# Gram products of every second row chunk made in the GIN stage, and rings of four buffers in the ranking stage of a four-layer graph network

## Chip, cores and metric

The kernel runs on one core of one Trainium2 chip. The metric is the device time of one execution in microseconds; smaller is better. TensorE (PE), VectorE (DVE), ScalarE (ACT), GpSimd (POOL) and SyncE (SP) have instruction queues of their own and meet by semaphores; 16 DMA engines move data.

## What is computed

Four graph layers, each followed by a residual and a row normalisation, over x of 50000 nodes x 256 features and 12500 edges. The change concerns the first layer (GIN) only:

```python
msgs = edge_vals[:, None] * x[edge_col]
agg = jax.ops.segment_sum(msgs, edge_row, num_segments=n)
h = (1.0 + eps[0]) * x + agg
h = _bn_relu(h @ W1 + b1, g1, be1)      # mean and variance over all 50000 rows
```

The batch norm needs the mean and variance of h @ W1. The kernel gets both from the Gram matrix of h, the 256 x 257 sum over all rows of h-transposed times [h, 1], before the matrix product itself is made. With h = s*x + agg, where agg is not zero only in rows that an edge ends in, the Gram matrix is the sum of the products of s*x with itself (all rows, the costly part) and of corrections for the rows with edges.

## The kernel before

The program runs phase by phase, and all engines meet between two phases: setup, histogram, ranking (function rank, 140 to 594 us of the profiled execution), segments (597 to 628), GIN edges (gin_edges, 628 to 1107), moments, then the matrix products and the other three layers, which the change doesn't touch.

The rows of x are cut into NCH = 100 chunks of 500 rows (125 partitions x 4 rows x 256 floats, 512 KB), the edges into T = 100 tiles of 125.

**Ranking** does two things side by side in one loop of 100 steps. It sorts the edges by source and by destination: VectorE makes one-hots of the keys' digits (L481) and copies of the keys (L484), TensorE transposes them (turn, L540 and L541), looks up the running table (find, L552) and adds the tile to it (count_in, L561), ScalarE copies and rounds the table (L444, L450) and the transposed one-hots (L457), VectorE compares keys in the tile (L493), makes the table's rest (L518) and sums of the lookup (L502), and GpSimd scatters the records by two indirect DMAs (L179). And it walks over x: SyncE loads chunk t into xin (L423), ScalarE scales it by 1 + eps into xc (L464), SyncE stores xc as H (L429, to the scratch tensor XP), and TensorE adds the chunk's products to gram in PSUM (moments, L572): for each of its 4 rows a partition two matmuls, one of 257 columns and one, for the second half of the features, of 129; the missing quarter is the transpose of another and is added once at the end (L467, L578). xin and xc have two buffers each. Every float32 matmul is recorded as two.

The order on every engine is that of its list in run_stages: step t runs each entry (lag, step) for tile t - lag, in the order of the list. In ranking TensorE has turn(t-1), find(t-3), count_in(t-1), moments(t-1); ScalarE copy_table(t-1), copy_hot(t-1), round_table(t-1), scale(t); VectorE find(t-4), one_hot(t), places(t-4), same_before(t-1), table_rest(t-2); SyncE store(t-2), load(t).

**GIN edges** runs over the 100 edge tiles and one more (the lead tile). GpSimd gathers the rows of x at both ends of the edges (xd and xs, L175) and scatters the finished rows to H (L179); ScalarE makes the messages (L716) and the scaled rows (L722), VectorE the running sums (L744), the emitted rows and the rest (L753 to L774), TensorE adds the corrections to gram, two matmuls of 257 columns a tile (L791). All rings have RING = 4 slots. SyncE has no work in this phase. GpSimd's list is write(t-3), fetch(t).

## Time and profile before

| | |
|---|---|
| median of 3 runs | 4572.68 us (4570.46 to 4578.47) |
| the profiled execution | 4575.74 us, its span 4573.1 us |
| busy share of the span | PE 75%, DVE 71%, POOL 64%, ACT 59% |
| mean granted clock of TensorE | 0.864 of full speed |
| HBM read and written | 352.28 MB and 339.16 MB |

The profile divides the span in 40 slices of 114.3 us. Each digit is the busy share of a slice in tenths (9 is 90% or more), PEclk the granted clock in tenths, DMA the mean busy share of the 16 DMA engines:

```profile
PE   4899934445999997999999777777566658850588
PEclk9999955555999998999999787777799979985799
DMA  1688823332444446888888333333333337753344
```

### The profile page before, as it was taken

To read this page: it belongs to the slowest core of one execution; us is meant where nothing else is said; L and a number is where in the kernel's file an instruction comes from. 1 tells how busy PE (TensorE), PEld (TensorE's weight loads), DVE (VectorE), ACT (ScalarE), POOL (GpSimd) and SP (SyncE) were. 2 spreads that over 40 slices of the span, in tenths; PEclk is the share of its full clock that TensorE was granted. 3 is DMA by queue.
4 is the path that set the end of the run, shared out by engine and by line. 5 is a ranking of instruction groups with operands and counts; after the bars stand their busy time and mean duration, and the time that the engine had idled before them with its cause. 6 is when DMAs were issued, how large, how long until landed. Compare 5 with 4: busy or idle time off the path is not lost. (4 is left out here: it accounts for less than half of the span.)

```text
span 4573.1 us, 92084 instructions
## 1 busy us (share of the span) xinstructions
PE 3430.6 (75%) x17524; PEld 2595.8 (57%) x17524; DVE 3237.9 (71%) x11747; ACT 2715.4 (59%) x6436; POOL 2914.7 (64%) x2826
## 2 busy tenths in 40 slices
PE   4899934445999997999999777777566658850588
PEld 2799922223888886666666555555466635530365
DVE  7788843334555556999999798999555587740798
ACT  0688812222666666989989588888555536640366
POOL 0366658885434443888888788887655537667476
PEclk9999955555999998999999787777799979985799
DMA  1688823332444446888888333333333337753344
GB/s 54 177 237 236 238 74 80 79 80 79 162 161 161 161 161 185 269 268 267 264 265 267 104 99 99 98 100 97 98 88 88 86 95 213 214 161 82 97 135 115
DMA packets 437548, 685.41 MB, mean 150 GB/s; under 512 B 171062, under 2 KB 284588, under 8 KB 437396
## 3 DMA queue, kind: packets, MB, share of 16 engines
q1 hardware_dynamic: 263572, 521.77, 37.2%
q0 software_dynamic: 173824, 162.17, 14.7%
q14 instruction: 124, 1.02, 0.1%
q8 instruction: 28, 0.46, 0.0%
HBM read 352.28 MB, written 339.16 MB: 151 GB/s over the span
## 5 line engine op out<-in xcount | busy, mean ns | idle before, releaser
L1097 POOL TENSOR_TENSOR mlp_r_parts<-mlp_r,mlp_r_parts 128x500 fp32r<-128x500 f32 x200 | 253.0, 1265 | 403.4 <-ACT mlp_r_parts L1083 394.3
L1238 PE MATMUL nodes_xp<-w_self,nodes_x3T 128*125 128x256 f32 x1600 | 444.0, 400 | 45.5 <-DVE nodes_elu L1346 45.5
L791 PE MATMUL gram<-gin_both,gin_am 125*128 125x257 f32 x404 | 205.8, 665 | 266.8 <-DVE gin_both L774 254.6
L1238 PEld LDWEIGHTS nodes_xp<-w_self,nodes_x3T 128*125 128x125 f32 x1600 | 268.3, 187 | 111.3 <-ACT nodes_x3T L1277 39.0
L791 PEld LDWEIGHTS gram<-gin_both,gin_am 125*128 125x128 f32 x404 | 118.1, 322 | 354.4 <-issue 323.2
L1122 DVE BATCH_NORM_STATS2 mlp_stats<-mlp_y 128x500 f32 (+1 forms) x200 | 136.3, 682 | 253.3 <-ACT mlp_y L1073 253.3
L179 POOL DMA_INDIRECT by_src<-rank_recs,rank_place x100 | 119.7, 1197 | 293.2 <-DVE rank_recs L512 292.6
L1392 POOL TENSOR_TENSOR nodes_v<-nodes_elu,nodes_x 125x512 f32<-125x512 f32 x200 | 253.4, 1267 | 79.1 <-ACT nodes_x L1270 44.6
L1036 PE MATMUL mlp_y<-mlp_hT,mlp_w 128*128 128x500 f32 x1200 | 296.6, 396 | 1.5 <-DVE mlp_hT L1113 0.8
L1036 PE MATMUL mlp_y<-mlp_r_parts,mlp_w 128*128 128x500 f32 x1200 | 287.4, 388 | 0.8 <-ACT mlp_y L1073 0.8
L572 PE MATMUL gram<-rank_xc 125*128 125x257 f32 (+1 forms) x1600 | 279.1, 328 | 0.0
L1935 PE MATMUL att_kq<-att_w_parts,att_xT 128*125 128x256 f32 x1200 | 176.0, 298 | 136.6 <-DVE att_xT L2006 136.6
L572 PEld LDWEIGHTS gram<-rank_xc 125*128 125x128 f32 x1600 | 249.2, 191 | 22.4
L1081 ACT ACTIVATE mlp_r<-mlp_y,affine 128x500 f32<-128x500 f32 x200 | 153.7, 768 | 178.9 <-PE mlp_y L1036 178.9
L1036 PEld LDWEIGHTS mlp_y<-mlp_r_parts,mlp_w 128*128 128x128 f32 x1200 | 225.3, 188 | 47.1 <-POOL mlp_r_parts L1097 1.1
L744 DVE SCALAR_TENSOR_TENSOR gin_acc<-gin_acc,same,gin_msg 125x256 f32<-125x256 f32 x100 | 48.4, 484 | 286.6 <-ACT gin_msg L716 205.7
L1384 POOL TENSOR_SCALAR nodes_x<-nodes_u,nodes_r,nodes_nm 125x256 f32<-125x256 f32 x400 | 217.7, 553 | 45.7 <-DVE nodes_nm L1339 33.9
L1935 PEld LDWEIGHTS att_kq<-att_w_parts,att_xT 128*125 128x125 f32 x1200 | 154.7, 194 | 158.8 <-DVE att_xT L2006 138.6
L1036 PEld LDWEIGHTS mlp_y<-mlp_hT,mlp_w 128*128 128x128 f32 x1200 | 218.1, 188 | 41.0 <-DVE mlp_hT L1116 1.1
L716 ACT ACTIVATE gin_msg<-gin_xd,srec 125x256 f32<-125x256 f32 x100 | 50.7, 507 | 316.0 <-DMA gin_xd<-x,other 316.0
L1251 ACT ACTIVATE nodes_z<-nodes_y,affine 128x250 f32<-128x250 f32 x400 | 215.2, 588 | 33.3 <-ACT nodes_r L801 18.0
L175 POOL DMA_INDIRECT att_xd<-XX,att_dst x100 | 121.4, 1214 | 159.0 <-issue 150.5
(426 smaller groups left out, 11951.3 us busy)
## 6 DMA issues: line engine op xcount, KB each, us to landing
XX<-mlp_y SPq DMA_DIRECT2D x100, 500.0 KB
nodes_y<-XX SPq DMA_DIRECT2D x100, 500.0 KB
rank_xin<-x SPq DMA_DIRECT2D x100, 448.0 KB
XP<-rank_xc SPq DMA_DIRECT2D x100, 448.0 KB
mlp_h<-XP SPq DMA_DIRECT2D x100, 448.0 KB
nodes_x<-x SPq DMA_DIRECT2D x100, 448.0 KB
XX<-nodes_x SPq DMA_DIRECT2D x100, 448.0 KB
out<-nodes_out SPq DMA_DIRECT2D x100, 448.0 KB
```

The costliest lines, as they stand in the source:

```text
L175: self.pool.indirect_dma_start(out, None, table, bass.IndirectOffsetOnAxis(index, 0)).then_inc(sem, 16)
L572: mm = pe.matmul(gram[:, m, 128 * m:F + 1], xc[:, s, j, 128 * m:128 * m + 128], xc[:, s, j, 128 * m:F + 1], start=False, stop=True, skip_g ...
L791: mm = pe.matmul(gram[:, m, 0:F + 1], am[:, s, 128 * m:128 * m + 128], both[:, s, 0:F + 1], start=False, stop=True, skip_group_check=True)
L1036: mm = pe.matmul(out[:, m, 0:CH], w[:, a, k, 128 * m:128 * m + 128], rows[:, s, b, k, :], start=((k, a, b) == terms[0]), stop=((k, a, b) = ...
L1081: act.activation(r[:, s, m, :], y1[:, m, 0:CH], ACT.Relu, bias=aff[:, 1, m:m + 1], scale=aff[:, 0, m:m + 1]).then_inc(s_r, 1)
L1097: pool.tensor_tensor(rp[:, s, 1, m, :], r[:, s, m, :], rp[:, s, 0, m, :], ALU.subtract).then_inc(s_rp, 1)
L1122: dve.bn_stats(stats[:, m, at.col, :].rearrange("p o n -> p (o n)"), y[:, s, m, :]).then_inc(s_st, 1)
L1238: pe.matmul(xp[:, b, j, :], x3T[:, s, k, P * j:P * j + P], w_self[:, k, 0:F], start=(k == 0), stop=False)
L1251: act.activation(z[:, s, m, :], y[:, c, m, HC * h:HC * h + HC], ACT.Relu, bias=aff[:, 3, m:m + 1], scale=aff[:, 2, m:m + 1]).then_inc(s_z, 1)
L1384: pool.tensor_scalar(x1[:, s, j, :], u[:, at.slot(LONG), j, :], r[:, s, 0, j:j + 1], nm[:, s, 0, j:j + 1], ALU.mult, ALU.add).then_inc(s_x ...
L1392: pool.tensor_tensor(v[:, at.slot(LONG), :, :], el[:, s, :, :], x3[:, at.slot(LONG), :, :], ALU.add).then_inc(s_v, 1)
L1935: mm = pe.matmul(out, xT[:, s, i, x0 + k, :], wp[:, j, k, w0:w0 + F], start=((k, i, j) == terms[0]), stop=((k, i, j) == terms[-1]), skip_g ...
```

## The change

In ranking xin and xc get four buffers in place of two, each with its own semaphore; the load of chunk t waits for the scaling of chunk t - 4, and the store stands four steps behind the load in SyncE's list. Products (moments) are made of the even chunks alone; the scaling still runs for all, and all are stored. In GIN every odd step handles one odd chunk: SyncE loads it a second time into one of two new buffers, ScalarE scales it three steps later (after that step's message and scaled rows), and TensorE adds its products four steps later, with both matmuls 257 columns wide, since the quarter that is mirrored at the end of ranking can't be mirrored here. VectorE sets the ones beside the new buffers, and TensorE waits for that once.

```diff
@@ rank
-    xin = ph.sb("xin", [P, 2, 4, F])
-    xc = ph.sb("xc", [P, 2, 4, F + 4])
+    xin = ph.sb("xin", [P, RING, 4, F])
+    xc = ph.sb("xc", [P, RING, 4, F + 4])
...
             def load(at):
-                s = at.slot(2)
-                wait(sp, s_xc, at.count(1, -1))
+                s = at.slot(RING)
+                wait(sp, s_xc, at.count(1, 1 - RING))
...
-            run_stages(sp, [(2, store), (0, load)], NCH)
+            run_stages(sp, [(4, store), (0, load)], NCH)
...
             def scale(at):
-                s = at.slot(2)
-                act.wait_ge(s_x[s], at.uses(2, 32, 32))
-                wait(act, s_h[s], at.uses(2, 32))
-                wait(act, s_gr, at.count(1, -1))
+                s = at.slot(RING)
+                act.wait_ge(s_x[s], at.uses(RING, 32, 32))
+                wait(act, s_h[s], at.uses(RING, 32))
+                if s % 2 == 0:
+                    wait(act, s_gr, at.uses(2, 1, -1))
...
             def moments(at):
-                s = at.slot(2)
+                s = at.slot(RING)
+                if s % 2:
+                    return
@@ gin_edges
+    xin, xc = ph.sb("xin", [P, 2, 4, F]), ph.sb("xc", [P, 2, 4, F + 4])
...
+    def odd_chunks(step):
+        return lambda at: step(at, at.slot(RING) // 2) if at.slot(2) and not at.is_lead else None
...
+            @odd_chunks
+            def load_chunk(at, b):
+                wait(sp, s_xc, at.uses(2, 1, -1))
+                for a, n in CUTS:
+                    sp.dma_start(xin[a:a + n, b, :, :], x_v[at.col, a:a + n, :, :].rearrange("o p j f -> (o p) j f")).then_inc(s_xl[b], 16)
+            run_stages(sp, [(0, load_chunk)], T)
...
-            run_stages(act, [(1, message), (1, scaled)], T + 1)
+            @odd_chunks
+            def scale_chunk(at, b):
+                act.wait_ge(s_xl[b], at.uses(RING, 32, 32))
+                wait(act, s_xg, at.uses(2, 1, -1))
+                act.activation(xc[:, b, :, 0:F], xin[:, b, :, :], ACT.Copy, scale=env["onep"][0:P, :]).then_inc(s_xc, 1)
+            run_stages(act, [(1, message), (1, scaled), (3, scale_chunk)], T + 1)
...
-            run_stages(pe, [(2, carry_over), (4, moments)], T + 1)
+            @odd_chunks
+            def chunk_moments(at, b):
+                pe.wait_ge(s_xc, at.uses(2, 1, 1))
+                for j in range(4):
+                    for m in range(KH):
+                        mm = pe.matmul(gram[:, m, 0:F + 1], xc[:, b, j, 128 * m:128 * m + 128], xc[:, b, j, 0:F + 1],
+                                       start=False, stop=True, skip_group_check=True)
+                mm.then_inc(s_xg, 1)
+            pe.wait_ge(s_init, 4)
+            run_stages(pe, [(2, carry_over), (4, moments), (4, chunk_moments)], T + 1)
```

## Rows read from the trace of the kernel before

**Rows 1.** Busy us of PE, PEld, DVE, ACT, POOL (instructions), PEclk, DMA share, GB/s.

```profile
200.00:550.00 350.00, 350.00 (x2709) 327.26 (x2708) 298.71 (x1355) 283.71 (x320) 213.10 (x160) 1.00 0.87 237
650.00:1100.00 450.00, 199.19 (x389) 114.40 (x390) 175.65 (x484) 97.48 (x192) 361.93 (x288) 0.50 0.32 80
```

**Rows 2.** Groups, 200 to 550 us: busy, mean ns | idle before, releasers.

```profile
L572 PE MATMUL gram<-rank_xc 125*128 125x257 f32 x640 | 191.5, 381 | 0.0
...
L464 ACT ACTIVATE rank_xc<-rank_xin,onep 125x1024 f32<-125x1024 f32 x80 | 92.0, 1150 | 33.3 <-DMA rank_xin<-x 33.1
...
L481 DVE TENSOR_SCALAR rank_hot<-iota_row,digit 125x256 bf16<-125x256 bf16 x320 | 70.0, 282 | 15.6 <-DVE rank_junk L502 9.8
...
L493 DVE SCALAR_TENSOR_TENSOR rank_junk<-rank_rows,keyf,before 125x125 f32<-125x125 f32 x159 | 49.1, 347 | 35.7 <-PE rank_rows L541 35.7
...
L457 ACT COPY rank_hotT<-rank_hT 128x500 bf16<-128x500 bf16 x80 | 46.0, 575 | 32.9 <-PE rank_rows L541 31.8
```

**Rows 3.** Tile rank_xc, 140 to 600 us: ns min/median/max, first and last start.

```profile
L464 ACT ACTIVATE rank_xc<-rank_xin,onep x100: 1147/1149/1161, 144.3 to 578.4; 125x1024 f32<-125x1024 f32 x100
```

**Rows 4.** TensorE in order of time in one ranking step: start, duration.

```profile
304.18 0.27 PE L540 MATMUL rank_hT<-ident_bf,rank_hot 125*128 125x125 bf16 x2
...
305.94 2.79 PE L572 MATMUL gram<-rank_xc 125*128 125x257 f32 x16
308.57 0.27 PE L540 MATMUL rank_hT<-ident_bf,rank_hot 125*128 125x125 bf16 x2
```

**Rows 5.** SyncE's own waits, 200 to 550 us: total us, times, longest.

```profile
SPq L429 <- ACT rank_xc L464: 63.8, 79, 1.5
```

**Rows 6.** DMA queues, 200 to 550 us: packets, MB, share of 16 engines.

```profile
q1 hardware_dynamic: 54606, 81.85, 82.7%
q0 software_dynamic: 5102, 1.14, 4.6%
```

**Rows 7.** Groups of GpSimd in GIN, 650 to 1100 us.

```profile
L175 POOL DMA_INDIRECT gin_xs<-x,node x96 | 127.0, 1323 | 29.3 <-issue 17.7 <-ACT gin_hs L722 11.3 <-ACT gin_msg L716 0.3
L179 POOL DMA_INDIRECT XP<-gin_hrow,write x97 | 119.7, 1234 | 29.6 <-issue 29.3 <-DVE gin_hrow L768 0.3
L175 POOL DMA_INDIRECT gin_xd<-x,other x95 | 116.0, 1221 | 29.0 <-issue 22.6 <-ACT gin_msg L716 6.4
```

**Rows 8.** Busy us, clock, DMA share, GB/s by window (columns of group 1).

```profile
1100.00:1105.00 5.00, 1.58 (x6) 0.68 (x4) 0.62 (x2) 0.00 (x0) 1.22 (x1) 0.84 0.18 49
1795.00:1800.00 5.00, 5.00 (x16) 3.56 (x16) 3.76 (x14) 4.79 (x12) 1.37 (x3) 0.51 1.04 238
1800.00:1805.00 5.00, 5.00 (x29) 3.51 (x28) 2.19 (x6) 4.79 (x12) 0.00 (x0) 1.00 1.03 284
...
3800.00:3850.00 50.00, 40.36 (x186) 26.06 (x186) 38.85 (x169) 31.37 (x117) 35.78 (x29) 1.00 0.77 215
```

**Rows 9.** DMA queue, 1850 to 2500 us (columns of group 6).

```profile
q1 hardware_dynamic: 51150, 172.86, 83.1%
```

**Rows 10.** Order of time inside GIN, 903 to 906 us.

```profile
903.21 0.42 DVE L768 TENSOR_TENSOR gin_hrow<-gin_acc,gin_hs 125x256 f32<-125x256 f32 x1
...
905.75 1.22 POOL L179 DMA_INDIRECT XP<-gin_hrow,write  x1 [0.30 <-issue]
```

**Rows 11.** Group of GpSimd in the attention sums, 3750 to 4050 us.

```profile
L179 POOL DMA_INDIRECT XP<-att_x_xp,write x86 | 106.1, 1234 | 62.3 <-ACT att_x_xp L2149 53.8 <-issue 8.5
```

**Rows 12.** Order of time at GIN's first product and at its end.

```profile
638.91 1.65 PE L791 MATMUL gram<-gin_both,gin_am 125*128 125x257 f32 x3 [12.19 <-DVE gin_am L760]
...
1096.89 3.58 PE L791 MATMUL gram<-gin_both,gin_am 125*128 125x257 f32 x8
...
1099.17 0.51 ACT L722 ACTIVATE gin_hs<-gin_xs,onep 125x256 f32<-125x256 f32 x1 [2.57 <-DMA gin_xs<-x,node]
...
1100.49 1.22 POOL L179 DMA_INDIRECT XP<-gin_hrow,write  x1 [1.09 <-DVE gin_hrow L768]
...
1107.15 0.69 DVE L819 COPY mom_g<-gram 128x514 f32<-128x514 f32 x1 [6.50 <-PEq L158]
```

More of the change, by code:

```diff
@@ L407, in rank @@
     gram = env["gram"]
-    s_x, s_h = ph.pair("x"), ph.pair("h_stored")
+    s_x, s_h = ([ph.sem(f"{n}{k}") for k in range(RING)] for n in ("x", "h_stored"))
     s_scat, s_scat2 = ([ph.sem(f"{n}{k}") for k in range(RING)] for n in ("scattered_a", "scattered_b"))
@@ L429, in store @@
                     sp.dma_start(h_v[at.col, a:a + n, :, :].rearrange("o p j f -> (o p) j f"), xc[a:a + n, s, :, 0:F]).then_inc(s_h[s], 16)
-            run_stages(sp, [(2, store), (0, load)], NCH)
-            for s in range(2):
-                sp.wait_ge(s_h[s], 32 * (NCH // 2))
+            run_stages(sp, [(4, store), (0, load)], NCH)
+            for s in range(RING):
+                sp.wait_ge(s_h[s], 32 * (NCH // RING))
         @block.scalar
@@ L459, in scale @@
             def scale(at):
-                s = at.slot(2)
-                act.wait_ge(s_x[s], at.uses(2, 32, 32))
-                wait(act, s_h[s], at.uses(2, 32))
-                wait(act, s_gr, at.count(1, -1))
+                s = at.slot(RING)
[3 more added lines that the diff above has]
+                    wait(act, s_gr, at.uses(2, 1, -1))
                 act.activation(xc[:, s, :, 0:F], xin[:, s, :, :], ACT.Copy, scale=env["onep"][0:P, :]).then_inc(s_xc, 1)
             run_stages(act, [(1, copy_table), (1, copy_hot), (1, round_table), (0, scale)], T)
-            act.wait_ge(s_gr, T)
+            act.wait_ge(s_gr, NCH // 2)
             act.copy(upper[:, :], gram[:, 0, 128:F]).then_inc(s_upper, 1)
@@ L470, in _ @@
         def _(dve):
-            for s in range(2):
+            for s in range(0, RING, 2):
                 dve.memset(xc[:, s, :, F:F + 4], 1.0).then_inc(s_one, 1)
@@ L566, in moments @@
             def moments(at):
-                s = at.slot(2)
+                s = at.slot(RING)
+                if s % 2:
+                    return
                 pe.wait_ge(s_xc, at.count(1, 1))
@@ L680, in gin_edges @@
     am, both, hrow = ph.sb("am", [P, RING, F]), ph.sb("both", [P, RING, F + 4]), ph.sb("hrow", [P, RING, F])
+    xin, xc = ph.sb("xin", [P, 2, 4, F]), ph.sb("xc", [P, 2, 4, F + 4])
+    s_xl, s_xc, s_xg = ph.pair("x_loaded"), ph.sem("x_scaled"), ph.sem("x_gram")
+    x_v = d["x"].rearrange("(c p j) f -> c p j f", p=P, j=4)
     cps = ph.ps("carried", [P, 512])
@@ L685, in gin_edges, with _ @@
                             "init", "carried"))
+    def odd_chunks(step):
+        return lambda at: step(at, at.slot(RING) // 2) if at.slot(2) and not at.is_lead else None
     with nc.Block() as block:
+        @block.sync
+        def _(sp):
+            @odd_chunks
[4 more added lines that the diff above has]
+            run_stages(sp, [(0, load_chunk)], T)
         @block.gpsimd
@@ L729, in _ @@
             dve.memset(both[:, :, F:F + 4], 1.0).then_inc(s_init, 1)
-            dve.wait_ge(s_init, 3)
+            dve.memset(xc[:, :, :, F:F + 4], 1.0).then_inc(s_init, 1)
+            dve.wait_ge(s_init, 4)
             def add(at):
```

## The prediction, made blind

> **What bounds the kernel now.** I read the stage table first: busy time, granted clock and DMA share of two stretches, ranking (200 to 550 us) and GIN (650 to 1100 us) [rows 1]. In ranking TensorE is busy 350.00 of 350 us at granted clock 1.00, its upper level, 2.4 GHz; VectorE 298.71, ScalarE 283.71, GpSimd 213.10, DMA share 0.87. In GIN no engine is full: GpSimd has 361.93 of 450, TensorE 199.19 at clock 0.50, which is 1.2 GHz, ScalarE 97.48, DMA 0.32. The change touches only these two stages and what lies between them.
>
> Then the groups of ranking with the idle time before them [rows 2]. TensorE has none before the Gram matmuls of L572, while VectorE waits 35.7 us for TensorE's transposes, ScalarE 31.8 us for the same and 33.1 us for the loads, over 80 steps. 80 scalings in 350 us are 4.375 us a step; all hundred start between 144.3 and 578.4 us, 4.385 a step [rows 3]. One step of TensorE in order of time [rows 4] gives its parts by their starts: transposes, table lookups and counting 304.18 to 305.94 (1.76), Gram products to 308.57 (2.63). Sum 4.39: the step is TensorE's, and 60% of it is the work that the change halves.
>
> In GIN the three indirect DMAs of a tile cost 1.221, 1.323 and 1.234 us on GpSimd, and each has about 0.3 us of plain issue before it [rows 7]: 3.78 + 0.90 = 4.68 us a tile, which is the stage's pace. No wait of weight lies on GpSimd.
>
> **Part 1: every second Gram block leaves ranking.** TensorE needs 4.39 in an even step and 4.39 - 2.63 = 1.76 in an odd one, on average 3.08. So TensorE stops setting the pace, and the next one does:
> - VectorE: 4.375 less its wait of 35.7/80 = 0.45 for TensorE is 3.93. Its busy time alone is 298.71/80 = 3.73; the 0.2 between is its own drain ahead of the one-hots (L481 waits for L502) [rows 2], which nothing in the change removes. 3.93 is my value, 3.73 the lower bound.
> - ScalarE: 283.71/80 = 3.55, below VectorE.
> - GpSimd: 213.10/80 = 2.66 and two issues of 0.3, 3.3 in all.
> - SyncE: it waited 63.8 us in 80 steps for the scaled chunk [rows 5], so it is occupied 4.375 - 0.80 = 3.58 with issuing.
> - DMA: 82.7% and 4.6% of 350 us over 80 steps are 3.62 + 0.20 = 3.82 us of every DMA engine a step [rows 6].
>
> Does an even step still cost 4.39? I followed the chain. The transposes of a tile start when VectorE has finished the previous tile's comparison (L493). VectorE then has all the rest of its step ahead of it before it wants the next transposes: 3.93 less two comparisons of 0.347 [rows 2], 3.2 us. After an even step TensorE is late by about 1.2 to 1.4 us (its lookup waits for the table rest, its counting for the table copy) and its odd step leaves over 2 us to catch up. So the 3.2 us cover the lateness, and the pace is VectorE's on both.
>
> **Part 2: four input and four output buffers.** Loads are issued once the scaling four chunks back is done, not two; the store of a chunk is issued with four chunks of lag in the list, still right after its scaling. The ring lets a load take about 16 us in place of 8. ScalarE's 33.1 us for loads would otherwise come into play once the step falls. It adds no bytes. What it can't do is make the DMA engines faster: at 3.93 us a step they would be booked 3.82/3.93 = 97%. Here is the unknown cost. The upper bound: in the start of a later stage (1795 to 1800 us) the engines were full, share 1.04, and moved only 238 GB/s [rows 8]; ranking's 237 GB/s [rows 1] over 4.375 us are 1.04 MB a step, which at 238 take 4.36 us, nearly today's step. The lower bound: in the next window the share was 1.03 at 284 GB/s, 3.65 us. I take 4.00 us a step: VectorE's 3.93 with a little lost to two resources this close together; it is nearest to the 3.82 that ranking's own rows show, and these were measured with the same packets. By the Trainium skill (DMA: Bandwidth & Descriptors, Specifications) a core gets some 358 GB/s from HBM; an estimate by that figure is 2.9 us a step, DMA would never bind and the step would be 3.93, 7 us better in all. No window here shows ranking above 240 GB/s on average, so I don't take it.
>
> Gain of the loop: 99 steps x (4.385 - 4.00) = 38 us. Bounds: VectorE's busy time 3.75, 63 us; DMA's 4.36, 2 us. The drain at the end of ranking has two more Gram blocks in a row (moments of chunks 98 and 99) ahead of the last lookups; without one of them about 2 us go, 0 to 2.6.
>
> **Part 3: the same products in GIN.** Added per odd chunk: one 512 KB load in two DMAs on SyncE, whose queue is empty in this stage; one scaling of 1.15 us on ScalarE (1149 ns, [rows 3]); 8 matmuls of full width 257, recorded as 16, on TensorE (before: four of 257 and four of 129). GpSimd, which sets the pace, gets nothing. Item by item:
> - ScalarE: 1.15 in 9.36 us, beside 21.7% busy. It stands last in a step's list, after the two scalings of the gathered rows. If it has to wait for its load, the next message (L716) waits behind it, then VectorE's sum, then GpSimd's scatter. The load is issued two chunks (about 18 us) ahead, so I cost it at nothing; if that cover went, all of the wait would land on GpSimd.
> - DMA: by the share and bytes of a stage with big rows, 83.1% of 650 us for 172.86 MB [rows 9], 512 KB take 1.6 us of every engine. The share of GIN goes from 0.32 to about 0.49. If a gather stands behind a whole chunk it lands 1.6 us later. What that may cost: the sum row is written at 903.21 + 0.42 = 903.63 and its scatter starts at 905.75 [rows 10], so 2.1 us of delay are free. Cost 0; upper bound 0.5 us in each second tile, 25 us, if queueing doubles the delay.
> - The same 16 engines carry both: the Trainium skill (DMA: Bandwidth & Descriptors, Issuing engines are not separate DMA queues) says that transfers interleave whoever issues them. This speaks against the change; by it a gather meets the 1.6 us worked out above, still under 2.1, so the sum is the same either way.
> - GpSimd's own instructions don't grow with DMA traffic: at share 0.77 [rows 8] in the attention sums a scatter takes 1.234 us, as in GIN [rows 11]. Cost 0, bound 0.03 us each, 9 us.
> - TensorE at the upper level: 24 records a pair of tiles, 16 of ranking's width take 2.63 for 193 columns on average, so 257 columns are 0.219 a record, 5.2 us in 9.36, 56%. At the lower level twice that, 10.4, which doesn't fit; see the third rival. Between them it has ring slots for four tiles and two chunks, so bursts are hidden.
> - The tail: the last chunk's scaling (99) stands on ScalarE behind the last gathered tile (hs at 1099.17 to 1099.68 [rows 12]). So chunk 99 is scaled at 1100.8, its 16 records end at 1104.3 (7.0 us if at the lower clock: 1107.8), and the last tile's products at 1105.2 or 1109.5. Today the next stage starts at 1107.15 after a scatter issued at 1100.49 [rows 12]; taking 2 us for the end of the stage (an estimate inside the 5.4 between the last scatter's end and that start), TensorE may run until 1105. Cost 0 to 5; I take 1.
>
> The four more semaphores to clear and the memset more have no row of their own; I cost them at nothing, 1 us at most.
>
> **Sum.** 38 + 2 - 1 = 39 us. The profiled execution is 4575.74 us (span 4573.1), 3 above the median of 4572.68; the saving is a difference inside one stage, so I take it from the median: 4572.7 - 38.7 = **4534 us**, 0.85% faster.
>
> **The rivals.**
> 1. The DMA engines become ranking's wall. For it: share 0.87 today, 0.97 wanted, and the 238 GB/s of full engines [rows 8]. Against it: ranking itself moves 237 GB/s at 0.87, which scales to 272 when full. A step of 4.08 to 4.36 gives gains of 30 to 2 us and the 1 of the ends: **4542 to 4570**, middle 4556. Chance 0.20.
> 2. GIN pays part of it: late gathers delay GpSimd's scatters in each second tile (25 us), or the tail is long. 4534 + 10 to 30: **4544 to 4564**. Chance 0.08. For it: the margin of 2.1 against 1.6 us is small. Against: the delay must hit the same pair of gathers each time.
> 3. Slower than before: TensorE stays at the lower clock in GIN. One pair of tiles then takes 10.4 us, 50 pairs 520 us, from the first product at 638.9 [rows 12] until about 1159. It may run until 1105 for nothing, so the stage ends 54 us later, in place of the 1 of the tail: 4534 + 53 = **4587**. It decides from a mean granted clock under 5.2/9.36 = 0.56. For it: GIN is at 0.50 today, and one window of another stage has 5.00 us of 5 busy at 0.51 [rows 8]. Against: the window right after that stands at 1.00, the eight records in a row at 1096.89 to 1100.5 are followed by 0.84 [rows 8, 12], and a TensorE that is late is never idle. Chance 0.04.
> 4. The change does not do what it says for the pace: an even step stays at 4.39 because one of TensorE's partners can't absorb it, and only odd steps fall to 3.95. Average 4.17: 4572.7 - 22 = **4551**, chance 0.05. Against: the 3.2 us of cover above.
> 5. Better than forecast, below 3.88 a step, because VectorE's drain hides in its waits: **4509 to 4522**, chance 0.04.
>
> **How the numbers follow.** The forecast (3.88 to 4.08 a step, 4522 to 4542) has 0.59. The range that should hold 8 in 10 leaves out the upper part of rivals 1 and 2, rival 3 and the edge of rival 5: 4518 to 4560. A measurement of this kernel can tell about 0.2% (9 us) from no change, so faster means under 4563.5: forecast 0.59, rival 5 0.04, rival 4 0.05, most of rivals 1 and 2 (0.24 of 0.28), 0.92, less 0.03 for what I did not think of: 0.89. Slower is rival 3, 0.04. The rest, 0.07, is within 0.2%.
>
> **What would show it.** Ranking: TensorE busy about 77%, VectorE near full, its wait on L541 gone from the list; starts of the scalings 3.9 to 4.1 us apart; DMA share 0.92 to 0.98 at 255 to 265 GB/s. If ScalarE or SyncE waits for loads while VectorE idles, it was rival 1. GIN: GpSimd's three instructions at 4.68 a tile with no new releaser, the stage as long as before to 3 us; DMA share near 0.49; granted clock between 0.6 and 1.0. A long wait of GpSimd's scatter for L768 would be rival 2, a TensorE always busy at 0.50 rival 3. The prediction is wrong if the ranking stage shrinks by under 25 or over 60 us, or GIN grows by over 10.

## The result, and the profile after

The changed kernel takes 4544.13 us (median of six, 4533.64 to 4552.14); the kernel before, run beside it, 4572.02 (4567.44 to 4578.47). The ratio is 0.9937, 95% interval 0.9920 to 0.9953: 28 us faster, where 39 were forecast, inside the range of 4518 to 4560 and 2 us above the 4522 to 4542 that were given to the forecast itself. The profiled execution of after took 4552.14 us (span 4549.2), the slowest of the six, so its total is not the one to read; its stages are.

The stage table first, the same columns as [rows 1].

```profile
200.00:550.00 350.00, 290.92 (x2229) 250.65 (x2228) 319.58 (x1455) 296.20 (x342) 207.44 (x173) 0.98 0.93 253
650.00:1100.00 450.00, 317.79 (x1158) 254.04 (x1159) 175.44 (x470) 138.65 (x227) 332.80 (x267) 0.85 0.49 129
```

In ranking TensorE is busy 290.92 of 350 us (83%, where 77% were forecast), no longer all of it. No other engine is full in its place: VectorE has 319.58, 91%. The DMA share has risen from 0.87 to 0.93. In GIN TensorE went from 199 to 318 us and its granted clock from 0.50 to 0.85, between its two levels of 1.2 and 2.4 GHz; the second window now reaches past GIN's end by some 25 us.

The start times of the hundred scalings (view by tile, columns of [rows 3]) give ranking's step, and those of the destination gathers and of the moments' first weight loads give GIN.

```profile
L465 ACT ACTIVATE rank_xc<-rank_xin,onep x100: 1147/1149/1167, 143.7 to 543.0; 125x1024 f32<-125x1024 f32 x100
L175 POOL DMA_INDIRECT gin_xd<-x,other x100: 1207/1220/1361, 593.5 to 1053.4; - x100
L880 PEld LDWEIGHTS mom_zp<-w,mom_g x8: 288/337/337, 1076.9 to 1079.6; 128*128 128x128 f32 x8
```

Before, the scalings ran from 144.3 to 578.4 [rows 3], and the other two lines were:

```profile
L175 POOL DMA_INDIRECT gin_xd<-x,other x100: 1211/1220/1241, 629.4 to 1090.3; - x100
L845 PEld LDWEIGHTS mom_zp<-w,mom_g x8: 288/337/337, 1108.0 to 1110.7; 128*128 128x128 f32 x8
```

So:

| stretch | before, us | after, us | gain | forecast |
|---|---|---|---|---|
| 99 steps of ranking | 434.1 (4.385 each) | 399.3 (4.033 each) | 34.8 | 38 |
| everything else up to the first gather | 195.3 | 194.2 | 1.1 | 2 |
| first to last gather of GIN | 460.9 | 459.9 | 1.0 | 0 |
| last gather to the next stage's first matmul | 17.7 | 23.5 | -5.8 | -1 |
| all later stages, which the change doesn't touch | 3465.1 | 3472.3 | -7.2 | 0 |

The last line is scatter of single executions: over all fourteen profiles of this study the later stages took between 3461 and 3472 us. Up to there the change gains 31.1 us, and the medians say 28.

Now the groups of ranking in the window 200 to 550 us, for comparison with [rows 2], and the waits of the same window (total us, times, longest).

```profile
L575 PE MATMUL gram<-rank_xc 125*128 125x129 f32 (+1 forms) x685 | 126.1, 339 | 0.0
...
L465 ACT ACTIVATE rank_xc<-rank_xin,onep 125x1024 f32<-125x1024 f32 x85 | 97.8, 1151 | 35.0 <-DMA rank_xin<-x 34.5
...
L494 DVE SCALAR_TENSOR_TENSOR rank_junk<-rank_rows,keyf,before 125x125 f32<-125x125 f32 x172 | 52.4, 341 | 14.0 <-PE rank_rows L542 13.1 <-DVE rank_recs L513 0.6
```

```profile
PEld rank_tab L562 <- ACT rank_table L444: 38.3, 41, 2.0
ACT rank_xc L465 <- DMA rank_xin<-x: 34.5, 51, 1.7
...
DVE rank_junk L494 <- PE rank_rows L542: 13.1, 9, 2.5
```

VectorE's wait for the transposes fell from 35.7 us in 80 steps to 13.1, but came in nine pieces of up to 2.5 us. Behind them is a chain that begins with a load: ScalarE's scaling waits 34.5 us for loads, the table copy behind it in ScalarE's list is late, TensorE waits 38.3 us for that copy, VectorE for TensorE. With four input buffers the loads should have been early. And the wait of [rows 5], SyncE's store for the scaled chunk, is gone: it was 63.8 us and is 0.4, and between 200 and 500 us SyncE's list of waits is empty. By the prediction's own test ("if ScalarE or SyncE waits for loads while VectorE idles, it was rival 1") this looks like DMA engines at their wall:

```profile
q1 hardware_dynamic: 58834, 87.15, 87.8%
q0 software_dynamic: 5548, 1.24, 5.4%
```

But an empty list of waits doesn't say that SyncE is free: its DMA issues are not counted as busy. The timeline of SyncE's queue (start, duration, line) shows it issuing nearly all the time:

```profile
300.18 1.98 SPq L423 DMA_DIRECT2D rank_xin<-x  x2
302.42 1.75 SPq L429 DMA_DIRECT2D XP<-rank_xc  x2
304.39 1.44 SPq L423 DMA_DIRECT2D rank_xin<-x  x2
306.01 1.74 SPq L429 DMA_DIRECT2D XP<-rank_xc  x2
```

So there are three candidates for the 4.03 us: the DMA engines' time, SyncE's issuing, and VectorE. VectorE's step where nothing disturbs it is 3.91: between 200 and 500 us it waits 9.0 us ahead of its comparisons (L494), 8.4 of them for TensorE, in 74.4 steps; that is 0.12 each, and 4.03 less 0.12 is 3.91. The experiments test the three one by one.

### The profile page after: what moved, and what is told of

Same layout as the page of the kernel before. It is cut to its first block and busy times, and to the rows that moved or that the text cites. A ratio compares the mean times of both kernels' runs of the same rounds, so it can differ in the third digit from the quotient of the medians.

```text
span 4549.2 us, 92731 instructions
## 1 busy us (share of the span) xinstructions
PE 3463.1 (76%) x17524; PEld 2631.5 (58%) x17524; DVE 3235.8 (71%) x11748; ACT 2761.0 (61%) x6486; POOL 2892.5 (64%) x2826
## 5 line engine op out<-in xcount | busy, mean ns | idle before, releaser
L825 PE MATMUL gram<-gin_xc 125*128 125x257 f32 x800 | 245.5, 475 | 133.0 <-ACT gin_xc L746 133.0
L825 PEld LDWEIGHTS gram<-gin_xc 125*128 125x128 f32 x800 | 189.1, 242 | 189.6 <-ACT gin_xc L746 153.1
L1434 POOL TENSOR_SCALAR nodes_out<-nodes_v,nodes_r,nodes_nm 125x256 f32<-125x256 f32 x400 | 220.9, 561 | 1.1 <-DMA out<-nodes_out 1.1
L1305 ACT ACTIVATE nodes_x<-nodes_u,nodes_nm,nodes_r 125x256 f32<-125x256 f32 x400 | 219.1, 599 | 0.0
L179 POOL DMA_INDIRECT out<-att_fin,write x101 | 124.7, 1235 | 94.9 <-DMA att_fin<-G 67.5
```

What stands on the lines that cost most here:

```text
L179: self.pool.indirect_dma_start(table, bass.IndirectOffsetOnAxis(index, 0), rows, None, bounds_check=self.bound, oob_is_err=False).then_inc ...
L825: mm = pe.matmul(gram[:, m, 0:F + 1], xc[:, b, j, 128 * m:128 * m + 128], xc[:, b, j, 0:F + 1], start=False, stop=True, skip_group_check=True)
L1305: act.activation(x3[:, at.slot(LONG), j, :], u[:, at.slot(LONG), j, :], ACT.Identity, bias=nm[:, s, 1, j:j + 1], scale=r[:, s, 1, j:j + 1] ...
L1434: pool.tensor_scalar(out[:, s, j, :], v[:, l, j, :], r2[:, l, j:j + 1], nm2[:, l, j:j + 1], ALU.mult, ALU.add).then_inc(s_out, 1)
```

## The experiments

What they measured, with the stretch of 200 to 500 us in the last three columns. From "changed with two buffers" on, each row is the changed kernel with the edit named. The step is the time from the first scaling to the last, divided by 99. "Issuing" is the sum of SyncE's DMA rows in the timeline; "SyncE waits" the sum of its waits.

| kernel | us | ratio (95%) | ranking step | DMA share, GB/s | issuing | SyncE waits |
|---|---|---|---|---|---|---|
| before | 4572.0 | 1 | 4.385 | 0.87, 237 | 212 | 54.2 |
| changed | 4544.1 | 0.9937 (0.9920 to 0.9953) | 4.033 | 0.94, 254 | 258 | 0 |
| changed, again | 4546.4 | 0.9939 (0.9922 to 0.9956) | 4.046 | 0.93, 251 | 258 | 0 |
| before + four buffers | 4577.2 | 0.9999 (0.9990 to 1.0009) | 4.366 | 0.88, 237 | 202 | 58.7 |
| changed with two buffers | 4584.7 | 1.0016 (1.0007 to 1.0026) | 4.425 | 0.87, 235 | 216 | 55.3 |
| odd products left out | 4537.8 | 0.9914 (0.9898 to 0.9931) | 3.989 | 0.93, 254 | 257 | 0 |
| GIN's tail reordered | 4542.7 | 0.9922 (0.9905 to 0.9938) | 4.033 | 0.93, 253 | 252 | 0 |
| lighter VectorE | 4548.9 | 0.9944 (0.9927 to 0.9960) | 4.070 | 0.91, 249 | 260 | 0 |
| odd stores in 4 KB rows | 4531.9 | 0.9916 (0.9899 to 0.9932) | 3.883 | 0.94, 266 | 239 | 23.5 |
| both of these | 4518.6 | 0.9886 (0.9868 to 0.9903) | 3.739 | 0.96, 277 | 238 | 15.9 |
| + one tiny DMA a step | 4592.2 | 1.0038 (1.0024 to 1.0052) | 4.481 | 0.85, 227 | 259 | 0 |
| 4 KB rows + tiny DMA | 4547.4 | 0.9942 (0.9925 to 0.9958) | 4.031 | 0.90, 252 | 257 | 0 |
| small load on ScalarE | 4542.2 | 0.9927 (0.9913 to 0.9941) | 3.908 | 0.95, 266 | 225 | 32.1 |
| 4 KB rows, lighter VectorE, tail | 4520.6 | 0.9880 (0.9863 to 0.9896) | 3.742 | 0.96, 276 | 243 | 9.6 |

The ratios are each against the runs of before on the same chip (4571.6 to 4576.8), so compare ratios or steps rather than microseconds between groups.

### The two halves of the change alone

Four buffers on the kernel before, TensorE's work unchanged:

```
-    xin = ph.sb("xin", [P, 2, 4, F])
+    xin = ph.sb("xin", [P, RING, 4, F])
...
-            run_stages(sp, [(2, store), (0, load)], NCH)
+            run_stages(sp, [(4, store), (0, load)], NCH)
```

> The kernel before with four buffers in ranking and nothing else moved: all Gram products stay there. Both theories say that TensorE sets the step (busy 350 of 350 us before), so more buffers buy nothing: step 4.38 us between starts of the scalings, total 4572 plus or minus 4 us. If the buffers alone were what made the change faster, the total would be 4540 to 4550.

ScalarE's wait for loads disappears from the list (33.1 us in [rows 2]) and what it waits for now is TensorE's transposes, 62.4 us. The time is the same, because TensorE is busy 300.00 of 300 us.

The changed kernel with two buffers in place of four:

```
-    xin = ph.sb("xin", [P, RING, 4, F])
+    xin = ph.sb("xin", [P, 2, 4, F])
...
-            run_stages(sp, [(4, store), (0, load)], NCH)
+            run_stages(sp, [(2, store), (0, load)], NCH)
```

> The changed kernel with the two input and two output buffers of the kernel before in ranking. Theory V (VectorE sets the changed ranking step of 4.03 us, 3.91 of its own and 0.12 lost when a load comes late): buffers only cover late loads, a load now gets 8 us, step 4.05 to 4.15, total 4546 to 4556. Theory D (the DMA engines or SyncE's issue set it, since SyncE never waits in the changed kernel): capacity matters, not depth, so also near 4.03 to 4.10 if two chunks in flight keep the engines full. A third view, that the ring is what carries the gain, wants 4.25 or more and a total above 4562.

It is a little slower than before although a third of TensorE's time in ranking is gone. Waits, 200 to 500 us:

```profile
ACT rank_xc L465 <- DMA rank_xin<-x: 49.9, 57, 2.2
PE rank_tab L562 <- ACT rank_table L444: 49.0, 36, 3.0
...
SPq L429 <- ACT rank_xc L465: 55.3, 65, 1.9
```

and ScalarE's scalings in the timeline, two steps of them, with the store and the load that SyncE issues behind the first:

```profile
299.68 1.15 ACT L465 ACTIVATE rank_xc<-rank_xin,onep 125x1024 f32<-125x1024 f32 x1 [0.68 <-DMA rank_xin<-x]
304.49 1.15 ACT L465 ACTIVATE rank_xc<-rank_xin,onep 125x1024 f32<-125x1024 f32 x1 [1.34 <-DMA rank_xin<-x]
308.12 1.15 ACT L465 ACTIVATE rank_xc<-rank_xin,onep 125x1024 f32<-125x1024 f32 x1 [0.16 <-DMA rank_xin<-x]
```

```profile
300.99 1.76 SPq L429 DMA_DIRECT2D XP<-rank_xc  x2
302.97 0.98 SPq L423 DMA_DIRECT2D rank_xin<-x  x2
```

This is a loop: scaling (to 300.83), then the store's issue (it waits for the scaling), the load's issue behind it (to 303.95), the landing some 4 us later, and the scaling two chunks on, at 308.12. It takes 8.44 us for two steps, 4.22 here and 4.43 on average. With two buffers this loop sets the pace as soon as TensorE doesn't, and the removal of the Gram blocks is worth nothing. Four buffers give the same loop four steps. Neither half gains alone; all of the gain comes from their being together.

### VectorE, and the size of the stores' pieces

First the changed kernel once more, to have it beside the others.

> The changed kernel as it is, on the same chip as the three below, to compare with: step of ranking 4.03 us between starts of the scalings, ratio to the kernel before 0.9937, some 29 us faster.

It gives the same step within 0.013 us and the same empty list of SyncE. Two more kernels below have the same ranking stage and change GIN alone; their steps are 3.989 and 4.033. So four executions of one ranking stage lie between 3.99 and 4.05, and a difference under 0.06 is not read here.

Then the changed kernel with less work for VectorE (one key copy for two, no copy of the records). By the durations of its instructions that is 0.3 us a step, by its busy time, in which they overlap, 0.15 to 0.2:

```
-                for key in range(2):
-                    dve.tensor_copy(keyb[:, s, key, :], keyf[:, key, at.col].broadcast_to([P, 128])).then_inc(s_keyb, 1)
+                dve.tensor_copy(keyb[:, s, :, :], keyf[:, :, at.col].broadcast_to([P, 2, 128])).then_inc(s_keyb, 2)
...
-                dve.tensor_copy(recs[:, s, :], env["rec"][:, at.col, :].rearrange("p o r -> p (o r)")).then_inc(s_place, 1)
```

> The changed kernel with 0.3 us a step taken from VectorE in ranking: both key copies in one instruction, and the records scattered from where they lie and not from a copy. Theory V (VectorE's own 3.91 us set the step, late loads add 0.12): step 3.75 to 3.85, total 20 to 28 us less than the changed kernel. Theory D (loads, through the DMA engines at share 0.94 and SyncE that never waits, set it): step stays at 3.98 to 4.05, total within 6 us of the changed kernel.

VectorE's busy time in 300 us falls from 276.49 to 259.19, and the step does not fall (4.070). Its wait for the transposes grows instead, from 8.4 us to 26.0. VectorE is not what holds the changed kernel at 4.03.

Next, odd chunks, whose products no longer need the column of ones beside them, get an output buffer of their own without that column. The row of a partition is then 4 KB in one piece and not four of 1 KB, and the bytes are the same:

```
-    xc = ph.sb("xc", [P, RING, 4, F + 4])
+    xc, xo = ph.sb("xc", [P, 2, 4, F + 4]), ph.sb("xo", [P, 2, 4, F])
...
+                    rows = xo[a:a + n, s // 2, :, :] if s % 2 else xc[a:a + n, s // 2, :, 0:F]
```

> The changed kernel with the odd chunks, which no product reads in ranking any more, scaled into rows without the gap for the ones, so that their stores are rows of 4 KB and not four pieces of 1 KB. DMA time of a step falls from 3.8 to about 3.6 us and SyncE's issue by 0.4. Theory V: the loss of 0.12 to late loads goes in good part, step 3.93 to 3.97, total 6 to 10 us less. Theory D: the step follows the DMA engines down to VectorE's 3.91, also 3.92 to 3.95; SyncE waits again. Alone it tells little, with the run above and the one below it tells the two apart.

The step falls to 3.883. The issue of a store shortens with the number of its pieces (view by line, ns min/median/max):

```profile
L430 SPq DMA_DIRECT2D XP<-rank_xo x78: 327/349/354, 202.1 to 499.6; - x78
L430 SPq DMA_DIRECT2D XP<-rank_xc x77: 651/909/928, 199.1 to 496.0; - x77
```

and SyncE waits for scalings again (13.2 + 10.3 us), while VectorE waits for no other engine between 200 and 500 us. The stage table has VectorE at 285.12 of 300:

```profile
200.00:500.00 300.00, 253.74 (x2000) 219.48 (x1999) 285.12 (x1307) 269.29 (x307) 182.47 (x154) 1.00 0.94 266
```

The same share of 0.94 as the changed kernel, at 266 in place of 254 GB/s. This run helps both remaining theories: fewer pieces shorten SyncE's issue and the DMA engines' time.

> Both edits, light VectorE and big rows of odd chunks. Theory V: step 3.62 to 3.70, the sum of both single gains or a little more. Theory D: the DMA engines' 3.6 to 3.8, step 3.70 to 3.85, far more than light VectorE alone gives, since each wall hides the other. Total 25 to 38 us less than the changed kernel.

With both edits the lighter VectorE pays at once: 3.739, lower by 0.144, and its busy time a step has fallen by 0.15. So with 4 KB rows the bound was VectorE, and without them it was not.

### SyncE's issuing against the DMA engines' time

The tests that tell the last two apart. One adds to SyncE's list of each step a DMA of 16 pieces of 8 bytes, which nothing reads:

```
-            run_stages(sp, [(4, store), (0, load)], NCH)
+            def extra(at):
+                s = at.slot(RING)
+                wait(sp, s_t[s], at.uses(RING, 16))
+                sp.dma_start(tiny[:, s, :], d["x"][0:16, 0:2]).then_inc(s_t[s], 16)
+            run_stages(sp, [(4, store), (0, extra), (0, load)], NCH)
```

> The changed kernel with one more DMA a step on SyncE in ranking, of 16 pieces of 8 bytes from the input into a buffer that nothing reads. It costs SyncE about 0.35 us of issue a step and the DMA engines almost nothing (128 bytes beside 1.04 MB). Theory A, SyncE's issuing sets the changed ranking step (it never waits there, and it is not shown as busy): the step goes from 4.04 to about 4.35 to 4.4, the time to 4575 to 4580. Theory B, the DMA engines' own time sets it (share 0.93 to 0.94), and SyncE's long issues are back-pressure of them: the step stays at 4.03 to 4.12, the time at 4545 to 4553.

The step rises to 4.481, by 0.45 us, even more than theory A said, and the kernel becomes slower than before. The DMA engines have less to do for it:

```profile
200.00:500.00 300.00, 235.97 (x1708) 201.24 (x1708) 244.21 (x1118) 227.47 (x262) 159.44 (x132) 0.93 0.85 227
```

Share 0.85, none of the compute engines above 82%, and ScalarE waits 60.2 us for loads. The edit adds 128 bytes and one instruction of SyncE's to each step, so the DMA engines' time alone did not set the step, and the order of issue on SyncE did. The three kinds of issue in that run:

```profile
L424 SPq DMA_DIRECT2D rank_xin<-x x130: 317/317/891, 202.5 to 496.5; - x130
...
L430 SPq DMA_DIRECT2D XP<-rank_xc x131: 656/897/898, 199.9 to 498.0; - x131
...
L434 SPq DMA_DIRECT2D rank_tiny<-x x66: 692/1285/2255, 200.9 to 498.9; - x66
```

The tiny DMA takes 1.285 us to issue and the loads behind it fall to 0.317 each, where in the changed kernel their median is 721 ns and their longest 1989. So it is not the load that is slow to issue but whatever is issued first behind the stores. In the kernel with 4 KB rows, by turns, the pair of loads behind the short stores is the long one:

```profile
299.90 1.85 SPq L430 DMA_DIRECT2D XP<-rank_xc  x2
301.98 1.32 SPq L423 DMA_DIRECT2D rank_xin<-x  x2
303.76 0.86 SPq L430 DMA_DIRECT2D XP<-rank_xo  x2
304.82 2.34 SPq L423 DMA_DIRECT2D rank_xin<-x  x2
```

Store and load together take 3.17 and 3.20 us. So part of the issue time is elastic.

The packets say what goes on meanwhile. In the changed kernel, while SyncE issues a pair of stores (298.21 to 299.96, first line) and then a pair of loads (300.18 to 302.16, second line), and in the kernel with the tiny DMA, while that one is in issue (254.35 to 256.02) and while the loads behind it are (256.24 to 257.06):

```profile
DMA packets 208, 0.50 MB, mean 285 GB/s; under 512 B 30, under 2 KB 105, under 8 KB 208
DMA packets 501, 0.49 MB, mean 246 GB/s; under 512 B 64, under 2 KB 489, under 8 KB 501
DMA packets 379, 0.38 MB, mean 225 GB/s; under 512 B 34, under 2 KB 372, under 8 KB 379
DMA packets 164, 0.09 MB, mean 111 GB/s; under 512 B 78, under 2 KB 164, under 8 KB 164
```

Packets of 4 KB are loads, those of 1 KB stores. During the stores' issue the engines still run 103 packets of the load before; during the long issue behind the stores they run the stores' pieces, nearly nothing else. With the tiny DMA in that place they have gone through most of the pieces by the time that SyncE comes to the loads, and fall to 111 GB/s. So the 3.46 us a step that SyncE spends issuing contain time in which it stands while the DMA engines work through small pieces. That the pieces are what it stands for is what these four stretches suggest; no run was made to show it.

The same edit on the kernel with 4 KB rows:

> The kernel with odd chunks stored in 4 KB rows (step 3.88, 4531.9 us, SyncE waiting 23.5 us in 300 us, 0.31 us a step) with the same small DMA a step. Theory A, SyncE's issuing: it has 0.31 us a step to spare here, the small DMA takes about 0.35, so the step stays at 3.88 to 3.95 (4532 to 4539) and SyncE's waits go. Theory B, the DMA engines: the step stays at 3.88 to 3.93 too, with SyncE's waits shortened by what the issue takes. If the step rises by over 0.15, the small DMA costs more than its issue, and the run before it can't be read as issue time alone.

The step rises by 0.148, above the 3.88 to 3.95 of theory A and the 3.88 to 3.93 of theory B, and just under the 0.15 that was set as the limit of the test, and not by the 0.35 or 0.45 of the issue: SyncE had 23.5/77 = 0.31 us a step to spare and used it up, 0.45 - 0.31 = 0.14. Its waits are gone. Theory A missed the size of the extra issue by 0.1 us, and with the size that the run before measured it gives this one to 0.01.

Last, the other way: SyncE relieved, and no byte or piece taken from the DMA engines. The 52 KB part of each load is issued by ScalarE.

```
-                for a, n in CUTS:
+                for a, n in CUTS[:1]:
...
+            def load_small(at):
+                s, (a, n) = at.slot(RING), CUTS[1]
+                wait(act, s_xc, at.count(1, 1 - RING))
+                act.dma_start(xin[a:a + n, s, :, :], x_v[at.col, a:a + n, :, :].rearrange("o p j f -> (o p) j f")).then_inc(s_x[s], 16)
+            run_stages(act, [(4, copy_table), (4, copy_hot), (0, load_small), (4, round_table), (3, scale)], T)
```

> The changed kernel with the same transfers, pieces and buffers, but the second DMA of each load in ranking (13 rows, 52 KB) is issued by ScalarE instead of SyncE. SyncE then has three DMAs a step to issue instead of four, at 0.32 us for the one that goes; ScalarE has one more (3.56 us busy of 4.03, and about 0.35 of issue). Theory A, SyncE's issuing sets the changed step: it falls by about 0.3, until VectorE's undisturbed 3.91 or ScalarE's 3.9 sets it: 3.85 to 3.95, and 4530 to 4539 us, with idle time of SyncE's queue ahead of its stores again. Theory B, the DMA engines' time at share 0.93 to 0.94 sets it: no byte and no piece is saved, so the step stays at 4.00 to 4.06 and the time at 4543 to 4550. Against both: if the step rises above 4.1, ScalarE's issue has become the bound.

The step falls to 3.908, VectorE's undisturbed 3.91, with SyncE waiting for scalings again and no wait of ScalarE for loads, nor of VectorE for another engine, in the window:

```profile
200.00:500.00 300.00, 253.52 (x2000) 220.25 (x1999) 284.96 (x1306) 271.77 (x307) 182.63 (x154) 1.00 0.95 266
```

```profile
SPq L429 <- ACT rank_xc L465: 32.1, 55, 1.3
```

```profile
L465 ACT ACTIVATE rank_xc<-rank_xin,onep x100: 1143/1155/1164, 149.7 to 536.6; 125x1024 f32<-125x1024 f32 x100
```

The same packets a step as in the changed kernel now move at 266 GB/s, so 254 was not the most that the DMA engines could do with them. One rival is left: the small load moves to a DMA queue of its own as well (q10, 4.10 MB, 5.3% in this window), so this run relieves SyncE's instruction list and SyncE's DMA queue together. No run parts the two; "SyncE's issuing" below means both. In total little is won (4542.2 us, the interval overlaps that of the changed kernel): the loop saves 12 us, but the first scaling starts 6.0 us later, at 149.7, behind one long wait of 8.6 us for loads: ScalarE issues its first four small loads only after its own start, at 143.39.

### GIN

The products of odd chunks left out of both stages:

```
-            run_stages(sp, [(0, load_chunk)], T)
...
-            run_stages(act, [(1, message), (1, scaled), (3, scale_chunk)], T + 1)
+            run_stages(act, [(1, message), (1, scaled)], T + 1)
...
-            run_stages(pe, [(2, carry_over), (4, moments), (4, chunk_moments)], T + 1)
+            run_stages(pe, [(2, carry_over), (4, moments)], T + 1)
```

> The changed kernel with the odd chunks' products left out altogether (no second load, scaling or product in GIN; the Gram matrix lacks the odd chunks). What falls away is the price of the GIN part. By the trace of the changed kernel the loop over the tiles costs nothing (first to last gather 459.9 us against 460.9 before) and the end of the stage 5 to 6 us, so the total should be 5 to 6 us below the changed kernel, near 4538. If the loads slowed GIN or a later stage, it falls by 10 us or more.

GIN's gathers then take 461.9 us from first to last, against 459.9 with the products (460.9 to 463.3 in the other runs that make them): the loop hides them all. From the last gather to the next stage it is 17.7 us, exactly as before, against 23.5. So the second load and the products cost the tail alone. (Of the nine runs with this GIN code seven have a tail of 23.4 to 23.6 us and two, the changed kernel's second run among them, one of 21.8. The cost is 4.1 to 5.9 us.) (Ranking's step came out at 3.989 here, 0.04 below the changed kernel, with nothing different in that stage; two executions of the changed kernel itself differ by 0.013.)

The tail in the changed kernel, in order of time:

```profile
1059.09 0.51 ACT L740 ACTIVATE gin_hs<-gin_xs,onep 125x256 f32<-125x256 f32 x1 [0.57 <-DMA gin_xs<-x,node]
...
1059.50 1.13 ACT L746 ACTIVATE gin_xc<-gin_xin,onep 125x1024 f32<-125x1024 f32 x1
...
1060.69 5.42 PE L825 MATMUL gram<-gin_xc 125*128 125x257 f32 x16 [3.77 <-ACT gin_xc L746]
...
1065.95 0.59 PE L808 MATMUL gin_carried<-gin_acc,carry 125*125 125x256 f32 x2
...
1066.68 0.42 DVE L764 TENSOR_TENSOR gin_acc<-gin_carried,gin_lead 125x256 f32<-125x256 f32 x1 [6.13 <-PE gin_carried L808]
...
1067.74 1.25 POOL L179 DMA_INDIRECT XP<-gin_hrow,write  x1 [6.68 <-DVE gin_hrow L793]
...
1068.98 3.63 PE L825 MATMUL gram<-gin_xc 125*128 125x257 f32 x16
```

The last carry (L808) and with it the last scatters stand behind the sixteen records of chunk 97, which take 5.42 us; chunk 99's come after them. VectorE waits 6.13 us for the carry, GpSimd 6.68. In the reordered kernel the chunk is scaled first in ScalarE's list and its products have a lag of two steps:

```
-            run_stages(act, [(1, message), (1, scaled), (3, scale_chunk)], T + 1)
+            run_stages(act, [(0, scale_chunk), (1, message), (1, scaled)], T + 1)
...
-            run_stages(pe, [(2, carry_over), (4, moments), (4, chunk_moments)], T + 1)
+            run_stages(pe, [(2, carry_over), (2, chunk_moments), (4, moments)], T + 1)
```

> The changed kernel with the odd chunk scaled in its own step (first in ScalarE's list) and its products two steps after it, ahead of the tile's corrections, in place of three and four steps. If the 5 to 6 us at the end of GIN come from the last two chunks' 32 records standing ahead of the lead tile's products on TensorE, they go: last gather to the start of the next stage back to 17 us from 23, total 4538. If they come from ScalarE or the loads, nothing changes.

The tail is 17.6 us (last gather 1056.9, moments 1074.5), its cost gone. The total, 4542.7, can't be told from that of the changed kernel, and neither can the loop's 462.6 us: the changed kernel's two runs have 459.9 and 463.1.

> Big rows, the lighter VectorE, and GIN's tail with the last chunk scaled first on ScalarE and its products taken ahead of the last carry. If the three gains are independent: ranking's step 3.74 as with the first two together (4518.6 us), last gather to next stage's first matmul 17.6 us in place of 23.5, so 4512 to 4514 us. Rival: the tail's gain is given back by the stages behind it, 4517 to 4520.

All three together: step 3.742, tail 17.8 us (1028.3 to 1046.1), and yet 4520.6 us (ratio 0.9880, 0.9863 to 0.9896) beside 4518.6 (0.9886, 0.9868 to 0.9903) without the tail's edit. The time is at the rival's 4517 to 4520, but the intervals of the two are 0.3% wide and a gain of 6 us (0.13%) can hide in them. In the profiled runs the next stage starts 4.2 us earlier and everything behind it takes 3470.6 us in place of 3462.4. Part of that can be seen in the traces. The 8 us ahead of the moments, with the tail's edit (first line) and without:

```profile
1038.00:1046.00 8.00, 2.38 (x5) 1.17 (x4) 1.37 (x3) 0.00 (x0) 1.23 (x1) 0.50 0.11 31
```

```profile
1042.00:1050.00 8.00, 4.89 (x23) 3.95 (x21) 0.91 (x2) 0.00 (x0) 1.58 (x2) 1.00 0.11 31
```

With the chunk's products moved forward, TensorE is busy 2.38 of 8 us and its granted clock is at 0.50, the lower level; with them last it is busy 4.89 and at 1.00. The moments then start at the lower one, and their eight first weight loads stretch over 2.7 in place of 1.4 us. This is not the reordering's doing alone: in the changed kernel's own trace, with the products last, the loads stretch over 2.7 us too, and in the kernel before. The other 7 us lie in the scatter of the later stages and stay open. Both kernels beat before by 1.1 to 1.2% and the changed one by 0.5%.

## Why the prediction was nearly right, and where it was not

**What bounds ranking before: right.** Four buffers alone changed nothing (ratio 0.9999) with TensorE at 300.00 of 300 us.

**The step of 4.00: right in size, in part by luck.** Measured 4.033 and 4.046. It was put together as VectorE's 3.93 and 0.07 lost to DMA engines at 97%. VectorE's part of this holds: its step undisturbed is 3.91, and 3.908 is what the kernel takes once SyncE is relieved. The 0.07 was a choice between bounds of 3.65 and 4.36 and stands near the measured 0.12 by luck. What fills the rest of the 4.03 is SyncE's issuing. The step that failed is the line on SyncE in part 1: occupied 4.375 - 0.80 = 3.58, and so below VectorE. The arithmetic was right, but the number was taken as a constant of the work. Counting issues alone it was 212/68.5 = 3.09 us a step before and 258/74.4 = 3.46 after, for the same four DMAs; with register and wait instructions, 4.03. The loads' part grew, from 96.2 to 128.2 us in 300, that is from 1.40 to 1.72 a step. In all seven kernels of the table whose SyncE has no wait, the sum of its issues stands at 252 to 260 us of 300, while their steps lie between 3.99 and 4.48; in the seven where SyncE waits, it is 202 to 243.

**The DMA engines' terms: not by themselves what set the step.** The upper bound of 4.36 was drawn from 238 GB/s of full engines [rows 8]; here 266 GB/s were reached with the same packets and 277 with larger ones. Their time a step, 0.94 x 4.033 = 3.79 us, agrees with the 3.82 worked out from [rows 6]. They are not out of the matter either: as the packets above show, SyncE's long issues fall where the engines run the stores' pieces.

**The rings: named, not priced.** Without them the step is 4.425, so they are worth 0.39 us of every step, all of the loop's gain. The text said that the wait for loads "would otherwise come into play once the step falls", which it does, and gave no price. That with two buffers the whole change would be worth nothing, it did not see. The chain could have been measured in the trace of before: from one scaling to the second next, through store issue, load issue and landing.

**The rivals.** Rival 1 by its sign (ScalarE waits for loads, VectorE idles) and by its time (4544, in 4542 to 4570) came true, by its step (4.08 to 4.36) and its mechanism not: a step made longer by 0.45 at share 0.85 and one made shorter by 0.12 at 0.95 both speak against a wall of the DMA engines alone. Its sign was too wide, since loads also come late when their issue is late. Rival 2: no late gathers; the loop of GIN kept its length and GpSimd's gathers 1220 ns. The long tail in it is real, 5.8 us. Rival 3: TensorE left the lower clock in GIN (0.85), as expected. Rival 4: its 4551 was missed; in the kernel with 4 KB rows and the lighter VectorE, with the same TensorE work, the scalings follow each other after 3.62, 3.96 and 3.55 us (301.19, 304.81, 308.77, 312.32), so no step stands at 4.39 there. Rival 5 did not come, though with two small edits more its 4509 to 4522 did (4518.6).

**GIN.** DMA share 0.49 as forecast, gathers undisturbed, 460 us. The tail was costed at 1 with bounds of 0 to 5; it was 5.8, and 4.1 in the changed kernel's second run. The text looked at chunk 99 alone and had its scaling as the start. What was late first was chunk 97's block of 16 records, in front of the last carry in TensorE's list. It took 5.42 us, at a mean granted clock of 0.68 between 1060 and 1065 us, against 3.63 for chunk 99's at 0.97 to 1.00.

**GpSimd, semaphores, memset: nothing, as said.** First scaling 144.3 before, 143.7 after.

**The sum.** Forecast 38 + 2 - 1 = 39. Measured up to the next stage 34.8 + 1.1 + 1.0 - 5.8 = 31.1, by the medians 28; the 3 between lie inside the scatter of the later stages. Three of the missing 8 are the step's 0.03 us, one the end of ranking, five the tail, and GIN's loop gave one back.

By the Trainium skill (DMA: Bandwidth & Descriptors, Issuing engines are not separate DMA queues) issuing from several engines only saves the sequencer's time to initiate a DMA, "which is usually small relative to the DMA itself". The runs agree with the first half: moving one small load to ScalarE left the DMA engines the same packets, and the step fell by 0.12 to 0.14 us, less than the 0.32 us of SyncE's that went. They differ on the second: in ranking initiating took SyncE 3.46 of 4.03 us, standing included, beside 3.79 us of the DMA engines.

## What to carry to other kernels

An engine that only issues DMAs can be the bound without a row in the profile's engine table that says so: it is counted as not busy, and in the seven kernels here that it held back it had no waits between 200 and 500 us. Add up its DMA instructions in the timeline, and watch for its waits to vanish; then count pieces and instructions, not bytes. When work is taken from the bounding engine, measure in the old trace the loop from a buffer's use to its next use, since fewer buffers than that loop needs can hold back the whole gain. In a pipelined stage that hides new work, look at the last two tiles by themselves: what stands ahead of the last dependent instruction is paid in full.

## What the runs showed of the hardware

- The issue time of a store on SyncE goes with its pieces: a pair of stores of 500 pieces of 1 KB takes 1.74 us, one of 125 pieces of 4 KB 0.86 us, with the same bytes.
- The DMA issued next behind such stores takes longer, whatever it is: 0.69 to 2.26 us for 16 pieces of 8 bytes, while the loads behind it take 0.317 us. The DMA share was 0.85 there; at 0.94 the changed kernel's loads, first of two behind the stores, took up to 1.99. While these long issues last, the engines run the stores' pieces (489 of 501 packets under 2 KB, 372 of 379). What the instruction waits for was not tested, and it stays open.
- With half of the stores in 4 KB rows the same DMA share of 0.94 went with 266 GB/s in place of 254. But the kernel with the small load on ScalarE moved 266 GB/s at 0.95 in 1 KB pieces, so the share alone doesn't tell how near the engines are to their limit.
- GpSimd's gathers of 125 rows took 1.220 us (median) in GIN, with the DMA share at 0.32 before and at 0.52 after (650 to 1050 us).
